# A decoder layer on one core: gate projection and mirrored sums moved into the convolution stage, a two-part transform, a written-out loop

## What is computed

```python
# block 1: gated long convolution ("S4D")
xz = einsum('bld,ed->bel', x, W_in); xc, z = split(xz, 2, axis=1)   # 512 + 512 channels
xc = silu(causal_conv_4_taps(xc, conv_w) + conv_b)
k  = 2 * einsum('hn,hnl->hl', Ct, exp(dtA[:, :, None] * t)).real     # kernel of 112 lags
y  = irfft(rfft(xc, n=224) * rfft(k, n=224))[..., :112] + xc * D
y  = y * silu(z);  x = layernorm(x + einsum('bhl,dh->bld', y, W_out))
# block 2: rmsnorm(x) @ W_x + b, plus a decayed sum of rmsnorm(ctx) rows picked by patch ends
x  = layernorm(x + xattn(x, ctx_2048, patch_lens))
# block 3: 8 experts, 256 -> 1024 -> 256, each token to the expert with the largest logit
x  = layernorm(x + ffn_of_chosen_expert(x))
```

## Time and profile before

| | us |
|---|---|
| median of 3 runs | 390.64 |
| lowest, highest | 390.28, 467.03 |
| the profiled execution | 386.12 |
| its span, first to last instruction | 384.2 |

### The profile page before, as it was taken

How to read it: one execution, slowest core, us unless ns; L and a number is a source line. 1 busy time by engine, 2 the same in 40 slices (tenths; PEclk the granted TensorE clock), 3 DMA queues, 4 the chain that set the end, 5 groups by cost and what they waited for, 6 DMA issues and landing times.

```text
span 384.2 us, 7410 instructions
## 1 busy us (share of the span) xinstructions
PE 331.1 (86%) x2078; PEld 276.4 (72%) x2079; DVE 241.8 (63%) x495; ACT 124.6 (32%) x335; POOL 216.6 (56%) x389
## 2 busy tenths in 40 slices
PE   1859968899999999999997613999999999999980
PEld 1435536668888888888886512899999999999970
DVE  6888999886897777777776558133443443443431
ACT  2558872702222222222221100234234234234220
POOL 6479980377776666666666204224465565565553
PEclk9969997899999999999999965899999999999996
DMA  7800000605444444444444065301001101001110
GB/s 227 306 1 3 0 0 0 200 25 160 151 135 132 131 130 130 130 141 131 139 145 131 26 265 206 143 12 43 29 28 32 38 27 41 28 20 41 36 40 23
DMA packets 17025, 34.84 MB, mean 91 GB/s; under 512 B 3456, under 2 KB 8455, under 8 KB 16360
## 3 DMA queue, kind: packets, MB, share of 16 engines
q1 hardware_dynamic: 14840, 29.88, 24.3%
q0 software_dynamic: 1872, 4.59, 4.0%
q10 hardware_dynamic: 288, 0.07, 0.1%
HBM read 30.86 MB, written 4.20 MB: 91 GB/s over the span
## 4 chain that ended last, share of the span: by engine, by line
PE 77%; DVE 10%; POOL 4%; issue 3%; ACT 2%; DMA 1%; DVEq 0%; POOLq 0%; ACTq 0%
PE ps L1344 17%; PE ps L1362 15%; PE ps L1212 7%; PE ps L1275 7%; PE ps L1257 7%; PE ps L1202 4%; PE ps L1154 4%; PE ps L1203 4%; PE ps L1295 3%; DVE w L893 2%; PE ps L1162 1%; PE ps L1299 1%; PE ps L1331 1%; POOL stage_b L580 1%; POOL stage_b L601 1%
## 5 line engine op out<-in xcount | busy, mean ns | idle before, releaser
L1344 PEld LDWEIGHTS ps<-stage_b 128*128 128x128 f32 x576 | 68.4, 195 | 2.6 <-DVE stage_b L1103 1.0
L1344 PE MATMUL ps<-stage_b 128*128 128x128 f32 x576 | 68.8, 279 | 1.2 <-ACT stage_b L819 1.2
L1362 PE MATMUL ps<-w,stage_b 128*128 x288 | 65.2, 380 | 0.7 <-DVE stage_b L1128 0.7
L1362 PEld LDWEIGHTS ps<-w,stage_b 128*128 128x128 f32 x288 | 53.3, 190 | 7.6 <-issue 1.1
L600 POOL TENSOR_TENSOR stage_b<-stage_b 112x512 f32<-112x512 f32 x16 | 21.1, 1321 | 44.1 <-DVE stage_b L949 24.2
L932 DVE TENSOR_SCALAR stage_b<-stage_b 112x256 f32<-112x256 f32 (+1 forms) x50 | 20.5, 410 | 35.0 <-POOL stage_b L668 21.8
L810 ACT ACTIVATE stage_b<-ps,b 128x128 f32<-128x128 f32 x144 | 39.3, 383 | 7.3 <-issue 7.2
L949 DVE TENSOR_TENSOR stage_b<-ps,w 112x512 f32<-112x512 f32 x64 | 39.6, 681 | 2.7 <-PE ps L1203 1.4
L640 POOL DMA_INDIRECT stage_b<-x_rows,stage_b x21 | 34.3, 1633 | 10.0 <-issue 5.9
L1212 PEld LDWEIGHTS ps<-w 128*128 128x128 f32 x256 | 32.9, 202 | 8.2 <-issue 6.9
L1103 DVE COPY stage_b<-w 128x2048 f32 x19 | 23.5, 1241 | 19.6 <-issue 14.0
(11 more groups left out here) (161 smaller groups left out, 517.5 us busy)
## 6 DMA issues: line engine op xcount, KB each, us to landing
w<-in_w SPq DMA_DIRECT2D x16, 512.0 KB, 3.9
w<-in_w SPq DMA_DIRECT2D x16, 256.0 KB, 2.9
w<-in_w SPq DMA_DIRECT2D x4, 1024.0 KB, 8.1
stage_b<-in_ctx SPq DMA_DIRECT2D x16, 224.0 KB, 2.9
w<-in_x_t SPq DMA_DIRECT2D x4, 448.0 KB, 5.8
stage_b<-in_x SPq DMA_DIRECT2D x16, 112.0 KB, 2.5
x_rows<-stage_b SPq DMA_DIRECT2D x16, 112.0 KB, 1.8
w<-in_w_in SPq DMA_DIRECT2D x2, 512.0 KB, 6.7
```

Of the source, the lines that this page charges most:

```text
L1344: last_ = m.matmul(ps[:, 2 * par + f // 4, (f % 4) * P:(f % 4 + 1) * P], w1_now[par][:, k, f * P:(f + 1) * P], rows_t[:, par, k * P:(k + 1 ...
L1362: last_ = m.matmul(ps[:, 4 + par, 0:D], h_t[:, par, f * P:(f + 1) * P], w2[:, e, f, :], start=(f == 0), stop=(f == FT - 1))
```

## The change

1. The gate projection leaves the sequence stage. 12 of its 16 units (448 columns each, `a_gate`) are computed inside the convolution stage, the last 4 in steps 0 to 3; ScalarE keeps all of silu(z) in `z_act`.
2. After silu, VectorE makes mirrored sums and differences of every sequence (`a_fold`, two operations a unit, both inputs in SBUF). The transform then works on 57 rows of sums (partitions 0 to 56) and 56 of differences (64 to 119), with two matmuls of K = 57 and K = 56 in place of two of K = 112. Spectrum and inverse transform have 120 rows, and the spectrum has four parts, not three.
3. Both loops are written out.
4. The reciprocal roots on GpSimd are three operations each, two columns wide; the context's root is made for two sequences at once. The normalising passes move from VectorE to ScalarE (three passes a sequence); the context's scale moves into `decay_b`; block 2's two sums become one (the matmuls accumulate in one bank).
5. Kernel phases are kept in turns, so that three VectorE passes over `theta` replace six.
6. The patch digits move behind the kernel sums, and the scan of 1792 becomes one of 256, with 13 small matmuls and ScalarE's relu.

The diff, cut to its core:

```diff
@@ ScalarE, convolution stage
+            for unit in range(UNITS):
+                a_unit(unit // HT, unit % HT)
+                if unit == 0:
+                    act.wait_ge(k_phase, K_PHASE)
+                    a.activation(theta, theta, ACT.Sin, scale=TWO_PI_BELOW).then_inc(k_sin, 1)
+                    for n in range(Z_EARLY):
+                        a_gate(n)
+                if unit >= HT:
+                    for n in gates_after(unit):
+                        a_gate(n)
@@ VectorE, convolution stage
+            def a_fold(unit, h):
+
+                x_now, to = conv_x[:, h % 2], folded[:, h % 2]
+                dve.wait_ge(act_x, unit + 1)
+                need(dve, xt_ps, unit - 1)
+                v.tensor_tensor(to[:, :, 0:HF + 1], x_now[:, :, 0:HF + 1], x_now[:, :, L:HF - 1:-1], ALU.add)
+                v.tensor_tensor(to[:, :, ODD:], x_now[:, :, 0:HF], x_now[:, :, L:HF:-1], ALU.subtract)\
+                 .then_inc(fold_set, 1)
...
+            for unit in range(UNITS):
+                a_step(unit // HT, unit % HT)
+                if unit > 0:
+                    a_fold(unit - 1, (unit - 1) % HT)
+            a_fold(UNITS - 1, HT - 1)
@@ TensorE, transform
-                    m.matmul(ps[0:L, 0, :], const("f_re", L), x_time[:, b, :], start=True, stop=True)
-                    m.matmul(ps[0:L, 1, :], const("f_im", L), x_time[:, b, :], start=True, stop=True)\
+                    m.matmul(ps[0:BINS, 0, :], const("fold")[0:HF + 1], x_time[0:HF + 1, b, :], start=True, stop=True)
+                    m.matmul(ps[0:BINS, 1, :], const("fold")[ODD:BINS], x_time[ODD:BINS, b, :], start=True, stop=True)\
                      .then_inc(dft_ps, 1)
@@ GpSimd, root of layer norm 1
-                    rsqrt(n_[:, 1:2], mv[0][par][:, 1:2], n_[:, 0:1], nr1_step, 5 * b).then_inc(nr1_step, 1)
-                    pool.wait_ge(nr1_step, 5 * b + 2)
-                    g.tensor_tensor(n_[:, 2:3], mv[0][par][:, 1:2], n_[:, 1:2], ALU.mult).then_inc(nr1_step, 1)
...
+                    g.tensor_tensor(ve[par][:, 0:2], var.to_broadcast([L, 2]), const("eps", L), ALU.add).then_inc(nr1_step, 1)
+                    pool.wait_ge(nr1_step, 2 * b + 1)
+                    g.tensor_tensor(n_[:, 0:2], ve[par][:, 0:2], m_half.to_broadcast([L, 2]), ALU.pow).then_inc(nr1_step, 1)
+                    apart(pool, (nr1_step, 2 * b + 2))
+                    g.tensor_scalar(n_[:, 2:4], n_[:, 0:2], mean, -1.0, ALU.mult, ALU.mult).then_inc(r1_set, 1)
@@ GpSimd, root of the context, only where par == 1 (every second sequence)
+                if b is not None and par == 1:
                     pool.wait_ge(sq_set, b + 1)
@@ ScalarE, sequence stage
+                    a.activation(x1_r[:, par, :], x1_pre[:, par, :], ACT.Identity, scale=nr[0][par][:, 1:2],
+                                 bias=nr[0][par][:, 3:4]).then_inc(x1r_set, 1)
+                    a.activation(x1[:, par, :], x1_pre[:, par, :], ACT.Identity, scale=nr[0][par][:, 0:1],
+                                 bias=nr[0][par][:, 2:3]).then_inc(x1_set, 1)
...
+                    act.wait_ge(decay_set, 1)
+                    act.wait_ge(cs_set, half + 1)
```

More of the change, by code:

```diff
@@ L38 @@
 NFFT = 2 * L
+HF = L // 2
+ODD = 64
+BINS = ODD + HF
 PT, PP = 3, 125
@@ L324, in b_steps @@
         def b_steps(engine, step):
-            for s in range(PRO):
-                step(s // 2, s % 2)
-            with engine.Fori(PRO // 2, NB // 2) as pair:
-                for q in range(2):
-                    step(pair, q)
-            for s in range(NB, NB + EPI):
+            for s in range(NB + EPI):
                 step(s // 2, s % 2)
@@ L1232, in _ @@
             transform(0, 0)
-            kernel_spectrum(0)
-            turn_kernel(1)
-            gate_input(0, 0)
-            for h in range(1, HT):
+            for h in range(HT):
                 kernel_spectrum(h)
@@ L1239, in _ @@
                     turn_kernel(h + 1)
+            a_gate(UNITS - Z_RAMP)
             pe.wait_ge(spec_set, HT)
+            pe.wait_ge(hits_set, 2)
+            for b in range(NB):
+                for k in range(PT):
+                    last = m.matmul(ps[0:LA, 7, b * LO:(b + 1) * LO], hit_hi[:, k * NB + b, 0:LA], hit_lo[:, k * NB + b, :],
+                                    start=(k == 0), stop=(k == PT - 1))
+            last.then_inc(at_ps, 1)
+            pe.wait_ge(at_set, 1)
+            pe.wait_ge(pick_set, 2)
+            full = ends_at.rearrange("p (b c) -> p b c", b=NB)[:, :, LO - 1:LO].to_broadcast([LA, NB, LO])
+            for a in range(LA):
+                o = ps[0:L, 4 + a // 2, a % 2 * NB * LO:(a % 2 + 1) * NB * LO]
+                last = m.matmul(o, pick[:, a, :], ends_at, start=True, stop=(a == 0))
+                if a > 0:
+                    last = m.matmul(o.rearrange("p (b c) -> p b c", b=NB), below[:, a, :], full, start=False, stop=True)
+            last.then_inc(count_ps, 1)
             pe.wait_ge(loaded["w_out"], 16)
@@ L1244, in step @@
             def step(pair, q):
-                if not (isinstance(pair, int) and (pair, q) == (0, 0)):
-                    for part in ((gate_input, transform) if isinstance(pair, int) and (pair, q) == (0, 1)
-                                 else (transform, gate_input)):
-                        part(pair, q)
+                if (pair, q) != (0, 0):
+                    transform(pair, q)
+                    b, par, half = seq(pair, q, 0)
+                    if b is not None and b < Z_RAMP:
+                        a_gate(UNITS - Z_RAMP + b)
                 b, par, half = seq(pair, q, 1)
```

425 lines of the change are left out of this document (212 added, 213 removed).

## The result

| | before | predicted | changed kernel |
|---|---|---|---|
| median | 390.08 | 375 | 392.37 |
| span of the profiled execution | 384.2 | 368.5 | 390.5 |
| ratio to before, 95% interval | | | 1.009 (1.007 to 1.012) |

The changed kernel is 0.9% slower, which is less than the 2% that counts as a difference here. The step of the sequence stage came out near the prediction. The stages ahead of it took back more than it gave. A few executions of any kernel are far longer than its others (467.0 of the kernel before, 680.5 of e8), and the ratios leave them out.

The account below looks back on a forecast made before the run. TensorE was taken to set the sequence stage's pace, 9.09 us a step. +9.7 up to transform 5, -20.9 over ten steps and -4.5 in the drain gave -15.7, so 390.6 became 375, own range 369 to 381.

Parts of the forecast that it names:

- The step: Sequence stage: mean step 7.0 us instead of 9.09, every second one 0.3 longer through ScalarE; -20.9 over ten.
- The pair: Transform's two half matmuls on TensorE: partly overlapping passes, three pass times, 1.3 us instead of 1.81.
- Convolution stage: Start to first kernel sum: lengthened by gate units, folds and their holds, to 71 us against 54.2.
- TensorE has 1.50, half a gate unit 0.75, and four transposes ...: 2.8 a unit: Convolution stage: TensorE's work per unit, transposes put at 0.55; with cold passes at unit 4 it gives 64.7.
- Only then comes the silu of unit 0: Convolution stage's start: first silu follows four gate units and ScalarE's last silu at 22.8; fold 0 starts at 23.5.
- The holds: Convolution stage: folds and GpSimd's outer products take turns, 1.7 us a fold pair, until GpSimd ends near 58.
- The ramp: First kernel sum to transform 5: 41.4 us, from 71.0 to 112.4, against 48.5 before.
- the list from "four kernel sums" to the decay operation: Ramp: kernel sums, digits, small matmuls, marks and scan, relus, exponential, decay operation in series, from 71.0 to 95.0.
- The drain: Transform 15 to the last logits: 26.5 us instead of 31.0, so -4.5 (-3 to -6).
- the cycle of 4.9: Drain: output projection, sum and statistics, root, ScalarE's pass, transpose make 4.9 us instead of 6.13; two cycles, -2.4.
- (c): Rival, convolution stage or ramp: folds wait for two products each time, or ramp equally later; +10, 385; chance 0.09.
- (d): Rival, sequence stage: VectorE's context product holds both pair sums, ring 8.8, with the context's root 9.2; 397; chance 0.05.

Follow-up runs that it names:

- e8: Changed kernel with x2's normalising pass on VectorE, behind the four products, instead of ScalarE; median 400.4, ratio 1.026.
- e12: e11 without the mirrored sums: two transform matmuls of 112 rows, the sums multiplied into their matrices; median 375.6, ratio 0.969.
- e1: Changed kernel with each convolution-stage gate unit ahead of the transposes on TensorE, not behind them; median 382.6, ratio 0.984.
- e13: Changed kernel with only the mirrored sums undone, multiplied into the transform's constants (two matmuls of 112 rows); median 380.3, ratio 0.982.
- e14: e13 plus e1's edit, the gate units ahead of the transposes on TensorE; median 378.9, ratio 0.981.
- e4: Changed kernel with both folds of a unit replaced by one operation on 4 columns, mirrored sums missing from the output; median 394.3, no ratio.
- e9: e5 with digits, hits, marks and scan moved into the convolution stage, gate unit 12 behind the counts, decay operation behind sequence 2's products; median 380.1, ratio 0.975.
- e11: e9 with marks and scan one unit sooner, ahead of the taps of unit 6 instead of unit 7; median 378.7, ratio 0.974.
- e5: e1 plus the four early gate silus moved behind the first convolution silu on ScalarE; median 382.2, ratio 0.978.
- e7: e5 with all work on the patch ends (digits, hits, marks, counts, relus) ahead of the kernel spectrum; median 386.6, ratio 0.993.
- e10: e9 with gate units 10 and 11 moved from ahead of the last transposes to between the kernel spectrum matmuls; median 388.4, ratio 0.996.

## Why the prediction was wrong, step by step

**The step: 7.0 predicted, 6.92 came, in part by luck.** It is 7.11 and 6.74 in turns, the longer one ended by ScalarE, as forecast. Sizes were off and cancelled. The pair takes 1.05, not 1.3: the half matmuls do not follow each other by passes as assumed, but their first passes run together and then their second. The rest of TensorE's step is 0.17 longer than beside a pair of 112 rows (e12), so that 6.74 stands against the 6.8 predicted. And ScalarE's passes over SBUF take 0.60, where 0.4 was put down from VectorE's pass, the wide power 0.70 to 0.76 instead of 0.55. The Trainium skill, "TensorEngine Tiling (Array Packing)", Key Properties, is borne out where it says that tiles run in parallel. For the drain that it tells of it has no size, and these rows leave room for little: the pair is 0.15 longer than half of 1.81, and 0.17 come beside it. What these 0.32 are was not tested apart.

**Convolution stage: 71, came 78.4. The failed step** is "TensorE has 1.50, half a gate unit 0.75, and four transposes ...: 2.8 a unit". It added up TensorE's work as if it could be done in any order, and compared it with VectorE's. Neither engine was full. In the stream, transposes that wait for the fold stand ahead of the gate unit and of the next projection, and so the times of both engines add up in a ring. The prediction had itself asked for this with the first gates ("Only then comes the silu of unit 0"), but not with the loop. e1, e13 and e14 show it: without the folds two units take 5.87, near twice the 2.8 that the sum gave. Of the 24.2 us by which the stage grew, 16.2 go with the folds (e13); the other 8.0 are still there without them, with the gates and the rest. Of the miss of 7.4, 1.3 lies ahead of the ring: fold 0 starts at 24.77, not 23.5, and the first sixteen passes end at 17.6, not 16.2.

**The holds: right in kind, too regular.** GpSimd's products ended near 56.5 (58 predicted), folds took 0.39 free and 0.9 held. That an operation waits for one product at most does not hold (e4, 7.28).

**The ramp: 41.4, came 51.9.** The failed step is the list from "four kernel sums" to the decay operation: 24.0 predicted, 29.8 measured (108.24 - 78.42). The hits are ready at 88.98, but the hit matmuls start at 92.94: they wait 4.0 for the last spectrum matmuls and for gate unit 12 (2.75), which the list did not have. The count matmuls take 2.75 instead of 1.9, the relus 2.66 instead of 1.93, and the decay operation 2.36, where the prediction had "2.0 with nobody in its way", because a pair sum ran beside it. The list had warm prices throughout, while TensorE got 0.67 of its clock from 90 to 100. The other 4.7 lie behind the decay operation (22.1 against 17.4), nearly all ahead of transform 4. The pair sum that it held took 3.05 and kept the products of sequence 2 waiting for 1.26; gate unit 14, also not in the list, stood ahead of the inverse transform until 110.42, and that took 3.13 instead of 1.94 at the lower clock. The rest of the 4.7 is not traced. e9 and e11 show that the serial list can be hidden: ramp 44.4 and 44.7. That the clock alone costs a certain part isn't settled; e5 against e1 gives 2 to 3 us, and the four equal ramps above differ by up to 4.2.

**The drain: 26.5, came 30.4.** Up to the last output projection it gained 3.7 of the 4.5 predicted. The terms in the cycle of 4.9, which came to 5.45, with hand-overs: output projection 1.93 (1.74 predicted), sum and statistics 1.18 (1.3), root 1.36 (1.1), ScalarE's pass 0.76 (0.5), transposes 0.22 (0.3). The larger failed term is one that was put at nothing: behind the last output projection 2.9 were lost (16.2 against 13.3). Block 2's last rounds are 5.18 and 6.15 apart (5.0 and 4.77 before), where a ScalarE pass of 0.60 stands in place of VectorE's 0.41 and the last matmuls are at the lower clock. This is read from the trace, not tested apart.

**The rivals.** (c), folds or a ramp that are later by 10, was the nearest in its sum, 385, for another reason. (d) did not come; e8 shows a neighbour of its mechanism. No rival had an engine's order as its subject.

## What to carry to other kernels

When work is added to a stage of several engines, write down for one unit the streams of all engines with their waits and look for rings; the sum of an engine's work is only a lower bound. Put what waits for nobody (here the gate unit) ahead of what waits. A saving in a full engine should be weighed against what it costs on the critical path of another stage: mirrored sums saved 3.8 us in ten steps and cost 16 before them, and as a matrix multiplied into the constants they cost nothing before the steps. And a stage that nobody edited can change by some us with the clock that it meets (ramps of 47.7 to 51.9 here), so a gain is to be read stage by stage and not from the total alone.

## What the runs showed of the hardware beyond what was expected

- Two float32 matmuls on different rows (57 and 56) run side by side pass by pass: starts 0.01 apart, 1.05 for the pair where the two of 112 rows take 1.79 to 1.81. Beside the pair, TensorE's step is 0.17 longer.
- A VectorE operation of 4 columns with both inputs in SBUF took 7.28 us beside back-to-back GpSimd operations, and one of 256 columns 3.38 beside a power and two pair sums; the same two take 0.15 and 0.41 alone. Between the same products another one of 4 columns took 0.15 (e4, 42.81), so the wait is not regular.
- A ScalarE pass of 112 x 256 from SBUF to SBUF took 0.60, VectorE's 0.41.
- A power on GpSimd took 0.69 to 0.76 two columns wide, 0.55 one column wide.
- The same eight spectrum matmuls took 1.13 or 2.06. In e7, where their chain with ScalarE's copies runs alone, the granted clock was 0.50 from 80 to 90; in e10, with gate unit 11 between them, the last three blocks took 1.13 each.
